# One of two h tiles turned by DMA in steps 8 to 27, and VectorE's second rounding as two instructions

## What is computed

```
xn = layernorm(u)                      # over 256 channels
s  = causal_conv(xn, k) + xn * D       # k: 128 taps per channel, from Lambda, log_dt, W
xq, wq = fp4(x), fp4(w)                # blocks of 16: scale = max|block| / 6, then round to the E2M1 grid
h  = silu(fp4(xn) @ fp4(w_gate).T) * (fp4(xn) @ fp4(w_up).T)       # 704 wide
g  = silu(fp4(h) @ fp4(w_down).T)      # back to 256
out = u + s * g
```

## Time and profile before

| | us |
|---|---|
| median of 3 runs | 553.1 (553.01 to 553.49) |
| profiled execution | 553.86 |
| its span | 552.1 |
| PE busy | 464.1 (84%) |
| DVE (VectorE) busy | 525.9 (95%) |
| ACT (ScalarE) busy | 383.8 (70%) |
| POOL (GpSimd) busy | 231.0 (42%) |
| 16 DMA engines, hardware queue | 49.0% of the span |

### The profile page before, as it was taken

How to read it: one execution, slowest core, us unless ns; L and a number is a source line. 1 busy time by engine, 2 the same in 40 slices (tenths; PEclk the granted TensorE clock), 3 DMA queues, 4 the chain that set the end, 5 groups by cost and what they waited for, 6 DMA issues and landing times.

```text
span 552.1 us, 12614 instructions
## 1 busy us (share of the span) xinstructions
PE 464.1 (84%) x4733; PEld 317.8 (58%) x4733; DVE 525.9 (95%) x684; ACT 383.8 (70%) x542; POOL 231.0 (42%) x330
## 2 busy tenths in 40 slices
PE   0003486688888899999999999999999999999996
PEld 0000343245555567776767676767676767675675
DVE  6899999999999999999999999999999999999987
ACT  6999687978888866666666666666666666665463
POOL 1899974545545551111111111133333333337770
PEclk9999979899999999999999999999999999999999
DMA  5990008144434157374846474646475665736999
GB/s 162 352 337 1 1 21 229 40 116 118 114 110 144 39 136 206 100 192 115 186 121 173 119 169 116 179 120 164 118 177 125 172 135 154 154 96 91 211 199 208
DMA packets 134690, 78.91 MB, mean 143 GB/s; under 512 B 41600, under 2 KB 134272, under 8 KB 134528
## 3 DMA queue, kind: packets, MB, share of 16 engines
q1 hardware_dynamic: 127360, 70.86, 49.0%
q0 software_dynamic: 7280, 7.34, 8.5%
HBM read 61.28 MB, written 16.12 MB: 140 GB/s over the span
## 4 chain that ended last, share of the span: by engine, by line
DVE 55%; issue 22%; PE 10%; POOL 7%; ACT 5%; DVEq 1%; DMA 0%; SPq 0%; ACTq 0%; POOLq 0%
DVE work L986 11%; DVE sm L944 11%; DVE work L981 9%; DVE work L1013 7%; PE ps L1385 6%; DVE ps L959 4%; DVE work L997 4%; DVE work L967 3%; DVE work L1021 2%; POOL xh L571 2%; DVE sm L951 1%; POOL work L576 1%; PE ps L1401 1%; POOL xh L583 1%; POOL xh L589 1%
## 5 line engine op out<-in xcount | busy, mean ns | idle before, releaser
L1385 PE MATMUL ps<-wgu,work 128*128 128x512 f16 (+1 forms) x1152 | 241.7, 365 | 19.8 <-DVE work L1013 18.7
L1385 PEld LDWEIGHTS ps<-wgu,work 128*128 128x128 f16 x1152 | 109.2, 98 | 132.0 <-issue 16.2
L715 ACT ACTIVATE work<-ps,con 128x704 f32<-128x704 f32 x64 | 54.2, 847 | 118.1 <-PE ps L1385 118.0
L1401 PE MATMUL ps<-wdh,work 128*128 128x256 f16 x704 | 87.2, 272 | 0.2 <-ACT work L710 0.2
L710 ACT COPY work<-ps 128x1408 f16<-128x1408 f16 x64 | 84.8, 1325 | 2.3 <-PE ps L1392 2.1
L556 POOL TENSOR_TENSOR gbuf<-gbuf,xh 128x256 f32<-128x256 f32 (+1 forms) x42 | 37.7, 926 | 91.0 <-DVE work L997 84.7
L967 DVE TENSOR_TENSOR work<-work,ps 128x960 f32<-128x960 f32 (+2 forms) x67 | 71.4, 1105 | 1.2
L981 DVE SCALAR_TENSOR_TENSOR work<-work 128x960 f32<-128x960 bf16 (+2 forms) x67 | 72.3, 1116 | 0.2 <-ACT work L730 0.2
L986 DVE SCALAR_TENSOR_TENSOR work<-work 128x1920 f16<-128x1920 bf16 (+3 forms) x36 | 69.8, 1938 | 1.2
L1401 PEld LDWEIGHTS ps<-wdh,work 128*128 128x128 f16 x704 | 65.6, 98 | 8.9 <-ACT work L710 0.4
L944 DVE TENSOR_REDUCE sm<-work 128x120 f32<-128x1920 f32 (+2 forms) x33 | 68.0, 2060 | 1.3
(11 more groups left out here) (160 smaller groups left out, 618.0 us busy)
## 6 DMA issues: line engine op xcount, KB each, us to landing
work<-kpad SPq DMA_DIRECT2D x64, 512.0 KB, 4.1
gbuf<-u_rev SPq DMA_DIRECT2D x4, 2048.0 KB, 18.4
work<-L_attn_u SPq DMA_DIRECT2D x32, 256.0 KB, 2.8
out<-gbuf POOLq DMA_DIRECT2D x7, 1024.0 KB, 14.9
work<-L_attn_u SPq DMA_DIRECT2D x1, 1024.0 KB, 13.4
out<-gbuf SPq DMA_DIRECT2D x3, 256.0 KB, 3.9
work<-L_ffn_w_down SPq DMA_DIRECT2D x1, 704.0 KB, 6.6
work<-L_ffn_w_gate SPq DMA_DIRECT2D x1, 640.0 KB, 4.6
```

The lines of the kernel that those rows point to most:

```text
L1385: last = T.matmul(p_gu[:, a:b], xT[par][:, t, c, :], wgu[:, part, c % 2, a:b], start=(n == 0), stop=(n == len(todo) - 1))
L1401: T.matmul(dst, hT[t][:, c, :], wdh[:, c, :], start=(c == 0), stop=False)
```

## The change

In steps 8 to 27 the odd tile of h (2it-3) is no longer turned by TensorE into PSUM and copied by ScalarE: SyncE issues a transposing DMA from `hilo` to `hT[1]` (function `h_transpose` on SyncE, semaphore `h_td`), between the first filter load of the step and the others, behind `hl_v` and `dn_p`. TensorE's `down` of these tiles waits for `h_td`, and VectorE's `h_parts` waits for `hT_p` and, where the tile was turned by DMA, `h_td`, before it overwrites `hilo`. The counts of the turned tiles are adapted (`turned_before`). VectorE's second rounding becomes two instructions, for h (with its own mark) and for x (which counts `x_r`); `h_parts` waits for the first, `x_parts` for the second. On ScalarE steps 4 to 7 are written out in place of a loop; on VectorE steps 4 to 9 and 28 to 29 are written out, and 10 to 27 stay a loop.

```diff
+        def by_dma(n):
+            return n % 2 == 1 and 2 * S_CONV - 4 <= n < 2 * S_TAIL - 4
...
+            def h_transpose(n, par):
+
+                sp.wait_ge(hl_v, n // 2 + 1)
+                sp.wait_ge(dn_p, n - 1)
+                sp.dma_start_transpose(hT[1], hilo[par][:, 1, :]).then_inc(h_td, 16)
...
+                for n in tiles[:1]:
+                    load_t(n, n % 2)
+                if by_dma(it * 2 - 3):
+                    h_transpose(it * 2 - 3, it % 2)
+                for n in tiles[1:]:
+                    load_t(n, n % 2)
...
-                if td:
+                if td and turned is None:
                     h_copy(it * 2 - 3, 1)
...
+                    dve.wait_ge(hT_p, turned[0])
+                    dve.wait_ge(h_td, turned[1])
...
-                last = round_b(pp, cols, own.n)
+                rounded = own.n
+                if ch:
+                    own.mark(round_b(pp, HB, rounded))
+                if x:
+                    round_b(pp, XH, rounded).then_inc(x_r, 1)
                 dve.wait_ge(tb_p, it + 1)
+                if ch:
+                    h_parts(it - 1, pp, turned=turned)
                 if x:
-                    last.then_inc(x_r, 1)
-                else:
-                    own.mark(last)
-                if ch:
-                    if x:
-                        dve.wait_ge(x_r, it + 3)
-                    h_parts(it - 1, pp)
-                if x:
-                    own.settle()
                     x_parts(it + 2, par)
...
-            loop(PEEL, NP - 2)
+            for it in range(PEEL, S_CONV + 2):
+                step(it, it % 2, True, True, True, turned=(it + S_CONV - 4, 16 * (it - S_CONV)) if it > S_CONV else None)
+            loop(S_CONV + 2, S_TAIL)
+            for it in range(S_TAIL, NP - 2):
+                step(it, it % 2, True, True, True, turned=(it + S_CONV - 4, 16 * (it - S_CONV)) if it == S_TAIL else None)
...
             def down(n, t, dst=None):
-                pe.wait_ge(hT_a, n + 1)
+                if by_dma(n):
+                    pe.wait_ge(h_td, dma_turns(n))
+                else:
+                    pe.wait_ge(hT_a, turned_before(n) + 1)
...
-                    h_transpose(it * 2 - 3, 1, par)
+                    if not by_dma(it * 2 - 3):
+                        h_transpose(it * 2 - 3, 1, par)
```

More of the change, by code:

```diff
@@ L243, in build @@
         hT_a = sem("hT_a")
+        h_td = sem("h_td")
         dn_p = sem("dn_p")
@@ L394, in groups_of, with turned_before, dma_turns @@
             return groups_before(it + 1) - groups_before(it)
+        def turned_before(n):
+            first, last = 2 * S_CONV - 4, 2 * S_TAIL - 4
+            if n <= first:
+                return n
+            return first + (n - first + 1) // 2 if n < last else n - (last - first) // 2
+        def by_dma(n):
+            return n % 2 == 1 and 2 * S_CONV - 4 <= n < 2 * S_TAIL - 4
+        def dma_turns(n):
+            return 16 * ((n - 1) // 2 - (S_CONV - 2) + 1)
         PEEL = 4
@@ L485, in _ @@
                     load_t(1, 1)
+                tiles = []
                 if it >= S_CONV:
-                    for n in range(2 * groups_before(it) + 2, min(2 * groups_before(it + 1) + 2, H // 4)):
-                        load_t(n, n % 2)
+                    tiles = list(range(2 * groups_before(it) + 2, min(2 * groups_before(it + 1) + 2, H // 4)))
+                for n in tiles[:1]:
[4 more added lines that the diff above has]
+                    load_t(n, n % 2)
             sp.wait_ge(cv_h, H // 4)
@@ L705, in x_copy, with h_copy @@
                 nc.scalar.copy(xT[par], p_xT).then_inc(x_tc, 1)
-            def h_copy(n, par, src=p_hT):
-                act.wait_ge(hT_p, n + 1)
+            def h_copy(n, par, src=p_hT, turned=None):
+                act.wait_ge(hT_p, (turned_before(n) if turned is None else turned) + 1)
                 after(act, dn_p, n - 1)
@@ L743, in y_copy, with step @@
                                      scale=con[:, C_CONV:C_CONV + 1]).then_inc(cv_e, 1)
-            def step(it, par, x, xn, gu, ch, td, a2=False, cv=0, c0=None, td1=True, late=False, more=None):
+            def step(it, par, x, xn, gu, ch, td, a2=False, cv=0, c0=None, td1=True, late=False, more=None, turned=None):
                 if td:
-                    h_copy(it * 2 - 4, 0)
+                    h_copy(it * 2 - 4, 0, turned=turned)
                 if a2 and not late:
@@ L897, in _ @@
                      more=15 if it == 2 else None)
-            with act.Fori(0, (S_CONV - PEEL) // 2) as q:
-                for par in range(2):
-                    step(q * 2 + (PEEL + par), par, True, True, True, True, True, a2=True)
+            for it in range(PEEL, S_CONV):
+                step(it, it % 2, True, True, True, True, True, a2=True)
             act.wait_ge(con_ok, 1)
@@ L903, in _ @@
                 for par in range(2):
-                    step(q * 2 + (S_CONV + par), par, True, True, True, True, True, cv=2 - par, c0=q * 3 + 2 * par)
+                    step(q * 2 + (S_CONV + par), par, True, True, True, True, True, cv=2 - par, c0=q * 3 + 2 * par,
+                         turned=q * 2 + (S_CONV + par + (S_CONV - 4)))
             for it in range(S_TAIL, NP - 2):
@@ L1013, in h_mult, with h_parts @@
                 V.tensor_tensor(vb[par][:, I * t:I * t + I], sg, p_gu[:, I:2 * I], ALU.mult).then_inc(h_v, 1)
-            def h_parts(p, par, only=(0, 1)):
+            def h_parts(p, par, only=(0, 1), turned=None):
                 own.settle()
-                after(dve, hT_p, p * 2 - 2)
+                if turned is None:
+                    after(dve, hT_p, turned_before(p * 2 - 2))
+                else:
+                    dve.wait_ge(hT_p, turned[0])
+                    dve.wait_ge(h_td, turned[1])
                 t0, t1 = only[0], only[-1] + 1
@@ L1215, in _, with step @@
             h_mult(1, 1, 0)
-            def step(it, par, x, gu, ch):
+            def step(it, par, x, gu, ch, turned=None):
                 pp = 1 - par
@@ L1253, in loop @@
                         own.n = q * (2 * per_step) + (start + par * per_step)
-                        step(q * 2 + (s0 + par), par, True, True, True)
+                        it = q * 2 + (s0 + par)
+                        step(it, par, True, True, True,
+                             turned=None if s0 < S_CONV else (it + (S_CONV - 4), it * 16 - 16 * S_CONV))
                 own.n = start + per_step * (s1 - s0)
-            loop(PEEL, NP - 2)
+            for it in range(PEEL, S_CONV + 2):
[3 more added lines that the diff above has]
+                step(it, it % 2, True, True, True, turned=(it + S_CONV - 4, 16 * (it - S_CONV)) if it == S_TAIL else None)
             step(NP - 2, 0, False, True, True)
@@ L1389, in h_transpose @@
             def h_transpose(n, t, par, dst=p_hT):
-                after(pe, hT_a, n if dst is p_hT else n - 1)
+                after(pe, hT_a, turned_before(n) if dst is p_hT else turned_before(n) - 1)
                 for c in range(NC11):
```

## The result

The changed kernel takes 550.52 us (median of 7 runs, 549.41 to 551.81) against 553.51 for the kernel before on the same chips: a ratio of 0.9946, 95% interval 0.9935 to 0.9957. The profiled execution is 550.52 us long around a span of 548.7 (before: 553.86 and 552.1). So it is faster by 3.0 us, and not by the 5.6 forecast; 550.52 lies above the range. In two later comparisons on other chips it was 550.21 and 550.02 against 553.8, so 3.6 to 3.8 us; 3.6 is the value I explain. The sum started from 553.1, the median of three runs; seven gave 553.51 and the later comparisons 553.8, so 0.4 to 0.7 us of the distance to 547.5 lies in that base and not in the gain. One run of e3 (2072.91 us) and one of e11 (2728.44) are left out of the comparisons.

The account below looks back on a forecast made before the run. The prediction took VectorE's own instruction list, about 14.33 us a step, as the bound; 5.3 us from steps 4 to 29 plus 0.3 from steps 1 to 3, together 5.6 off 553.1, gave 547.5 us, range 546.6 to 549.8.

Parts of the forecast that it names:

- (1): VectorE's second rounding split in two, steps 4 to 29: waits pass under the x part, 0.205 us a step, 5.3 saved.
- (3): Waits in front of `h_parts`: own count, `hT_p` and `h_td` are over by 1.93 to 1.96 us, covered until 2.15.
- Rival A: Waits before `h_parts` not covered in the loop; the 18 looped steps keep half: 549.3 us, chance 0.12.
- (2): Written-out steps 1 to 3: smaller gap before `h_parts`, 0.10 us a step, 0.3 saved.
- (4): New wait `h_td` on VectorE: turn takes 1.7 us to issue, at most 4.3 to land; nobody waits for it.
- (6): SyncE's filter loads behind the turn: cost 0, bound above 0.95 us in each of 10 steps with two groups.
- Rival B: Second filter load of two-group steps comes behind the turn and TensorE waits: 557.0 us, chance 0.06.
- (5): TensorE loses 11 turns; two-group steps fall from 14.91 to 14.30 us; gains nothing itself, lets the split's saving through.
- (8): ScalarE drops a 1.33 us copy off the path; steps written out on ScalarE and VectorE cost nothing: 0.
- Rival C: VectorE's two roundings don't overlap, 2.37 to 2.43 us against 2.355: 1 us lost, 554.1 us, chance 0.04.
- Rival D: Gain shows nowhere because another engine sets the pace at once, ScalarE's silu being late: 553 us, chance 0.04.

Follow-up runs that it names:

- e3: The changed kernel without GpSimd's seven adding stores and the wait for them at the end: 548.53 us (0.9904).
- e11: The kernel before with the last x turn (step 30) made by TensorE in place of DMA: 553.47 us (1.0001).
- e6: The changed kernel with the second rounding as one instruction again, so the DMA turns and written-out steps alone: 556.31 us (1.0035).
- e5: The kernel before with only the second rounding split in two and the waits behind it edited, all loops as before: 551.95 us (0.996).
- e4: The changed kernel with the last x turn replaced by a plain copy of the same bytes on the same queue: 548.44 us (0.99).
- e9: The changed kernel with VectorE's steps 4 to 7 looped again and the last x turn made by TensorE: 548.29 us (0.9905).
- e2: The kernel before without GpSimd's seven adding stores and the wait for them at the end: 552.67 us (0.9981).

## Why the prediction was right and wrong

(1) and (3), the split in the loop, are right to 0.01 us a step: 2.15 from rounding to `h_parts`, 14.12 a step where 14.13 was said, 3.7 us in 18 steps. The three waits fit under the x part, as argued from the earlier trace rows; e6 shows them uncovered, and at the price given to `h_td`, 0.1. Rival A did not come.
(2) Steps 1 to 3: 0.35 against 0.3. Right, with some luck: this stretch alone scatters by 0.3 us between profiles of one kernel.
(4) and (6): turns land in 3.7 us at the median, nobody waits for one in the changed kernel, and TensorE's waits for filter loads are 0.4 us in all. Rival B did not come.
(5) is right in its mechanism and, by e5, in its size: without TensorE's relief two steps last 28.41 us where 28.4 was said, and every second step is 0.17 longer.
(8) and the 0.205 taken for steps 4 to 9 failed together by 0.7 us. (8) said that steps 1 to 3 are written out and show no gap; but the earlier trace rows give only the spot before `h_parts`. The end of a written-out step was also in the trace and wasn't read: L944 starts 0.10 us after `h_mult` there and 0.03 in the loop. That is 0.35 us in the five ends of steps 4 to 8 (step 9 ends into the loop). About 0.2 is silu in step 9: `h_mult` starts 0.39 us late behind it, against 0.19 in the kernel before, so the step keeps its 14.60. The rest, 0.1 to 0.2, is the lengthened L1009 of the even steps, open. Writing the steps out is the smaller part of the miss: e5 keeps the loop and takes 85.74 us for steps 4 to 9, only 0.08 less than the changed kernel, because there the even steps lose in L981 what they save at their end. So the term was mis-sized, 0.6 at most for what 1.2 was put down, mostly for reasons that (8) doesn't name.
The sum itself failed in its last line: "A gain of 5.6 us is taken off both". It assumed that the end follows VectorE at a fixed distance. The trace of before had DMA shares of 1.1 to 1.2 from 504 us to VectorE's end and a last x turn that took 10.5 us to land, the maximum in a row that I quoted for its median. The distance is set by the DMA engines (e3, e4 and e9 bring it to 2.2 us), and it grew by 1.1 us (3.0 to 4.1 at the mean of three profiles). The tail was no term of the sum, and no reason was given for leaving it out; that it has a price is shown, what makes it grow is open. Measured for the sum: 5.6, less 0.7 in steps 4 to 9, less 1.1 to 1.5 in the tail, is 3.4 to 3.8; measured 3.0 to 3.8.
Rival C has no support: two independent roundings take 2.15 us to the next start and not 2.37, and a wait costs 0.1 us when it stands behind the end of an instruction (e6) and none when it stands beside one. The Trainium skill (VectorE: DVE Perf Modes, "The DRAIN you can't avoid") says that the next operation waits for the pipe to empty, but adds that one that is not held starts earlier; the prediction left that out, and the overlap of 0.085 us agrees with the section as a whole. Its other statement, that the semaphore costs nothing extra, was measured there on a row of copies; for a wait behind the end of an instruction e6 disagrees, by 0.08 us a step. Rival D did not come either: silu was late once, by 0.3 us.

## What to carry to other kernels

A wait costs VectorE some 0.1 us of its own list even when it has long been met (0.09 and 0.11 in the earlier trace rows, 0.08 in e6), if it stands behind the end of the instruction before it; splitting that instruction so that an unrelated part runs while the waits pass is worth more than the 0.07 us that one more instruction costs (2.23 us for the pair, 2.16 for the one). Moving work off an engine that isn't the bound brought nothing alone here and cost a wait, but it may be what lets another saving through, so measure the two halves alone and together. And before a saving is taken off the end, read what the last transfers wait for: where the DMA engines are full in the tail, look for whatever opens a hole in their stream.

## What the runs showed of the hardware that I had not expected

A transposing DMA of 128x1024 float16 lands in 3.1 us without GpSimd's adding stores (e2, e3) and in 10.5 to 11.9 amid them, and all traffic falls from about 200 GB/s to 40 to 110 for up to three us around its landing; as a plain copy of the same bytes it leaves no such hole (e4). The turn of 128x1408 takes 1.38 us to issue and that of 128x1024 takes 1.23 (e3), so the queue's time grows by less than the blocks, 1.12 for 1.375. The same opening code runs with a granted clock of 1.00 or of 0.71 from 85.6 to 91.5 us, which moves everything behind it by 1.1 us.
